# Values of six chunks computed with their router logits beside the shared expert, stored, and loaded in attention

## The chip, the cores and the metric

The kernel runs on one core of a Trainium2 chip. The metric is the device time of one execution in microseconds, the median over several. A profiled execution comes with it: its span is the time between the first and the last instruction that the profiler recorded.

## The reference

The input x is (4, 1024, 256) in float32, so there are 4096 tokens of width 256. Cut to what matters:

```python
xn = (x - mean(x)) / sqrt(var(x) + 1e-5)              # over the last axis

# attention, one head of width 256, softmax over all 1024 keys of a batch
q = xn @ Wq.T + bq ; k = xn @ Wk.T + bk ; v = xn @ Wv.T + bv
z = softmax(q @ k.T / 16) @ v

# mixture of experts on the same xn: 16 experts of hidden width 128, the best 2 of each token
gates = softmax(xn @ Wg.T) ; scores, inds = top_k(gates, 2) ; scores /= sum(scores)
y = sum over the 2 of scores * (silu(xn @ We_gate[e].T) * (xn @ We_up[e].T)) @ We_down[e].T
# shared expert of hidden width 512, scaled by a gate of its own
shared = (silu(xn @ Ws_gate.T) * (xn @ Ws_up.T)) @ Ws_down.T
out = x + z + y + sigmoid(xn @ Wsg.T) * shared
```

## The kernel before

The 4096 tokens are 32 tiles of 128 rows, or 8 chunks of 4 tiles (a chunk is also a group g of 512 queries; two groups make one batch). Every float32 product is made of float32r halves: an operand is split into a high part and a remainder (`HI`, `LO`), and `product` (line 803) issues three passes for each half of the contraction, so six matmuls for a width of 256 and 24 for the 1024 keys.

There is no scheduler. `plan()` (line 103) writes one list of steps by hand. Each engine's program walks that list and issues what belongs to it in that order; semaphores carry the dependences. So the list sets each engine's order, and an engine that waits in one step holds up all its later ones.

The stages, in order:

- **Shared expert.** Steps 0 to 45 of `shared`, each a pair of gate and up products (`gate_up`, 12 matmuls of 512 columns) or a pair of tiles of the down projection (`down`, `down_second`, 24 matmuls of 256 columns). The table `beside` hangs the small work on them, in three places of a step: ahead, amid, behind. Among it: `tokens_in` (8 transposes of a chunk's normalized rows into `xT`), `logits` (4 matmuls of 512 columns with the router, padded to 128 columns, as the stationary operand, into a transposed form), `logits_turn` (4 transposes back, the two halves of the sum added by VectorE, DVE), `best_experts`, and then the routing itself. `expert_split` splits the experts' weights as they arrive, on ScalarE (ACT, high part) and GpSimd (POOL) or DVE (remainder). `xT` of each chunk is stored to `keys` in device memory.
- **Routed experts.** 79 blocks of 128 gathered rows, in 40 pairs (`blk_turn`, `blk_gate_up`, `blk_hidden`, `blk_down`). At its end stands the first work of attention.
- **Attention.** `heads` (b, u) makes the mixed queries of 512 tokens (12 matmuls of 512 columns), `values` (b, u) the values of four tiles (24 matmuls of 256 columns), both from `xT` loaded back as `xbT`. A group g has four pairs of key tiles: `scores` (g, pair), 12 matmuls of 512 columns, and `scores_copy` on ACT; `scores_max` on DVE finds the greatest key for each query, `tops` shifts it and POOL reduces it over the partitions, `spread` and `less` subtract it on DVE, `probs`, `probs_hi` (ACT) and `probs_lo` (DVE) make the weights of a tile of queries, and `weigh` (24 matmuls of 258 columns, 256 values and the sum) with `weigh_sum` on DVE ends it. A group's `weigh` stands one group later. `rows` is the sum of the routed experts' rows on DVE (`rows_in`), followed on POOL by the gather of the rows of the tile three further on into the same of three buffers (`YR`), which waits for that `rows_in`.

`scores_copy` of pair 0 of a group waits for all four `less` of the group before. `heads`, `values` and `scores` share two pairs of PSUM banks in turn (`ring_banks`). `tokens_in`, `logits`, `logits_turn` and others share two single banks in turn (`turn_bank`): a step waits until the one before it in its bank has been read. `weigh` (n) waits for `weigh_sum` (n-2) before it overwrites its bank.

Of the kernel before, what the change touches and what calls it, by code (L numbers as in the profile page):

```python
# [18 lines left out]
P = 128  # L19
# [3 lines left out]
KD = D // P  # L23
# [15 lines left out]
RLO = 32  # L39
# [63 lines left out]
def plan():  # L103
# [31 lines left out]

    shared = []
    for c in range(NCH):
        shared += [(up, c, 0), (up, c, 1)]
        if c > 0:
# [11 lines left out]
        3: ([], [], [("stats", 4)]),  # L151
        4: ([("weights_lo", 5)],
            [("logits", 1), ("logits_turn", 0), ("weights_hi", 5), ("root", 2, 3), ("invert", 2, 3)],
            []),
        5: ([("logits_turn", 1), ("best_experts", 0)], [], []),
# [3 lines left out]
        9: ([], [("tokens_in", 3), ("stats", 7)], []),  # L159
        10: ([], [("logits", 2)], []),  # L160
        11: ([("expert_load", 1), ("root", 4, 5, 6, 7), ("logits", 3), ("invert", 4, 5, 6, 7)],
            [("logits_turn", 2)],
            []),
        12: ([("norm", 4)], [], [("logits_turn", 3)]),
        13: ([], [("tokens_in", 4)], [("norm", 5), ("expert_split", 1)]),
        14: ([], [("logits", 4)], []),
        15: ([("norm", 6)], [("tokens_in", 5)], [("expert_split", 2)]),
        16: ([], [("tokens_in", 6), ("norm", 7)], []),
        17: ([("logits", 5)], [("logits_turn", 4), ("best_experts", 1)], []),
        18: ([("tokens_in", 7)], [("expert_split", 3)], []),  # L170
        19: ([("logits_turn", 5), ("logits", 6)], [], [("best_experts", 2)]),
        20: ([], [("logits_turn", 6), ("logits", 7)], [("expert_split", 4)]),
        21: ([], [("logits_turn", 7)], [("best_experts", 3)]),
# [33 lines left out]
    for b in range(PAIRS + 2):  # L207
        if 0 < b < PAIRS:
            steps.append(("blk_gate_up", b))

        if b == PAIRS:
            steps.append(("heads", 0, 0))
        if 0 < b <= PAIRS:
            steps.append(("blk_hidden", b - 1))
        if b == PAIRS + 1:
            steps.append(("values_first", 0, 0))
# [29 lines left out]
    ahead = {1: split("heads", 1, 1), 2: split("heads", 2, 0), 3: split("heads", 2, 1), 4: split("heads", 3, 0),  # L246
# [10 lines left out]
    for g in range(GROUPS):  # L257
# [18 lines left out]
        if g in (1, 3):  # L276
            steps.append(("keys_load", g // 2 + 2))
# [85 lines left out]
def build(nc, x, bv, Wqkv, bqk_in, Wr, We, Ws, const_f, const_b, out):  # L363
# [4 lines left out]
    with ctx:  # L368
# [230 lines left out]
        def inverse_of(c):  # L599

            return 5 * [c in group for group in ROOTS].index(True) + 4
# [1132 lines left out]
```

## Time and profile before

| | |
|---|---|
| median of 3 runs | 510.38 us (509.88 to 511.83) |
| profiled execution, its own time | 509.88 us |
| its span | 508.1 us |
| PE busy | 502.8 us |
| DVE busy | 402.9 us |
| ACT busy | 279.9 us |
| POOL busy | 197.9 us |

Busy time is the union of an engine's instructions. Matmuls are pipelined and overlap in it, so what one costs is read from the distance between starts, not from its duration. A piece of the chain of waits gives when it began, how long it lasted, and what ran; a bracket in a timeline row is the engine's idle time before the row and what ended it.

### The profile page before, as it was taken

Reading aid. Unit: us, or ns where it says so; the run is one execution under the profiler, and the core shown is the slowest. Engines: PE = TensorE matmul, PEld = TensorE weight load, DVE = VectorE, ACT = ScalarE, POOL = GpSimd, SP = SyncE. Lnnn points to the kernel's source line nnn. Section 1 sums busy time; section 2 is a strip of 40 time slices with the busy share of each in tenths; the row PEclk is TensorE's granted clock in tenths of the full one; section 3 lists DMA queues with packets and bytes.
Section 4 is the critical chain, followed back from the end, with each engine's and each line's share of the span. In section 5 each row is a group of like instructions: output and inputs, shape, how many; then the busy total and the mean of one; then the engine's idle time right before and its main releaser. Section 6 shows DMA issues by size and latency. Waiting matters only on the chain.

```text
span 508.1 us, 9935 instructions
## 1 busy us (share of the span) xinstructions
PE 502.8 (99%) x3411; PEld 461.3 (91%) x3411; DVE 402.9 (79%) x847; ACT 279.9 (55%) x466; POOL 197.9 (39%) x178
## 2 busy tenths in 40 slices
PE   8999999999999999999999999999999999999997
PEld 6898988888889999999999889999989898989897
DVE  6989457899997677677776288997969797887997
ACT  4787884246655465555555547473826454553652
POOL 0001021111005777777760370454363436262740
PEclk9999999999999999999999999999999999999999
DMA  8937176111213565786575740632253323121212
GB/s 303 411 133 281 79 288 243 42 54 33 62 63 109 179 190 181 228 305 205 188 153 137 249 137 21 199 112 63 85 159 122 83 62 84 33 78 47 82 55 74
DMA packets 31185, 71.27 MB, mean 140 GB/s; under 512 B 5313, under 2 KB 9793, under 8 KB 30113
## 3 DMA queue, kind: packets, MB, share of 16 engines
q1 hardware_dynamic: 23840, 51.80, 28.6%
q0 software_dynamic: 6864, 18.75, 14.4%
q8 instruction: 30, 0.49, 0.4%
q10 hardware_dynamic: 432, 0.09, 0.1%
q14 instruction: 19, 0.15, 0.1%
HBM read 43.34 MB, written 27.28 MB: 139 GB/s over the span
## 4 chain that ended last, share of the span: by engine, by line
PE 89%; DVE 7%; issue 2%; ACT 1%; DVEq 0%
PE ps L808 55%; PE ps L1018 11%; PE ps L948 7%; PE ps L814 6%; PE ps L1050 6%; PE ps L903 1%; PE ps L861 1%; PE ps L965 1%; DVE pT L1334 1%; DVE acc L1431 1%; PE ps L912 1%; DVE place_hot L1523 1%; DVE sil L1412 1%; DVE hT L1334 1%; DVE probs_f L1675 0%
## 5 line engine op out<-in xcount | busy, mean ns | idle before, releaser
L795 POOL DMA_INDIRECT rows_y<-ytab,slot x64 | 81.1, 1267 | 87.6 <-DVE acc L1690 67.9
L765 POOL DMA_INDIRECT blk_x<-rows,row x79 | 83.7, 1059 | 48.4 <-DVE row L1538 22.7
L808 PEld LDWEIGHTS ps<-vv,pT 128*128 128x128 f32 x768 | 94.6, 189 | 1.3 <-DVE pT L1334 0.3
L808 PE MATMUL ps<-vv,pT 128*128 128x258 f32 x768 | 95.6, 283 | 0.1
L808 PE MATMUL ps<-xT,shared_w 128*128 128x512 f32 x384 | 92.7, 394 | 0.4 <-DVE sil L1412 0.2
L808 PEld LDWEIGHTS ps<-xT,shared_w 128*128 128x128 f32 x384 | 70.7, 188 | 15.5 <-issue 0.8
L808 PE MATMUL ps<-qT,xbT_hi 128*128 128x512 f32 x256 | 79.1, 390 | 0.0
L1018 PE MATMUL ps<-expert_w,blk_xT 128*128 x474 | 66.0, 288 | 0.3 <-DVE blk_xT L1334 0.3
L1018 PEld LDWEIGHTS ps<-expert_w,blk_xT 128*128 128x128 f32 x474 | 58.9, 190 | 0.6 <-issue 0.6
L1322 ACT ACTIVATE probs_f<-probs_f 128x1024 f32<-128x1024 f32 x32 | 33.8, 1057 | 41.3 <-DVE probs_f L1675 41.2
L1128 ACT ACTIVATE scored_t<-ps 128x1024 f32<-128x1024 f32 (+1 forms) x33 | 32.4, 996 | 43.6 <-PE ps L808 39.4
L808 PEld LDWEIGHTS ps<-qT,xbT_hi 128*128 128x128 f32 x256 | 47.0, 188 | 9.2
L749 POOL TENSOR_TENSOR expert_w<-stage_e,expert_w 128x768 fp32r<-128x768 f32 x7 | 13.4, 1911 | 105.6 <-ACT expert_w L1128 105.6
L808 PE MATMUL ps<-qT,xbT_lo 128*128 128x512 f32 x128 | 50.0, 390 | 0.0
L1334 DVE TENSOR_TENSOR blk_xT<-ps,blk_xT 128x512 fp32r<-128x512 f32 (+1 forms) x40 | 27.3, 683 | 20.0 <-ACT blk_xT L1128 20.0
L948 PE MATMUL ps<-shared_w,hT 128*128 128x256 f32 x336 | 42.8, 285 | 0.0
L948 PEld LDWEIGHTS ps<-shared_w,hT 128*128 128x128 f32 x336 | 41.2, 191 | 0.2
L1334 DVE TENSOR_TENSOR pT<-probs_f,pT 128x1024 fp32r<-128x1024 f32 x32 | 39.1, 1223 | 0.8 <-ACT pT L1128 0.8
L1675 DVE TENSOR_TENSOR probs_f<-scored_t,less_wide 128x1024 f32<-128x1024 f32 x32 | 38.5, 1220 | 0.4
L1050 PE MATMUL ps<-expert_w,blk_hT 128*128 x237 | 38.0, 296 | 0.0
L1128 ACT ACTIVATE pT<-probs_f 128x1024 fp32r<-128x1024 f32 x32 | 33.9, 1059 | 0.8
L1252 ACT ACTIVATE blk_sil<-ps 128x256 f32<-128x256 f32 (+1 forms) x40 | 15.3, 382 | 32.9 <-PE ps L1018 32.9
(167 smaller groups left out, 858.2 us busy)
## 6 DMA issues: line engine op xcount, KB each, us to landing
ytab<-blk_y SPq DMA_DIRECT2D x40, 256.0 KB, 2.8
keys<-xT SPq DMA_DIRECT2D x8, 1024.0 KB, 6.1
stage_e<-in_experts SPq DMA_DIRECT2D x16, 384.0 KB, 3.1
rows<-xn SPq DMA_DIRECT2D x8, 512.0 KB, 3.2
xbT_hi<-keys SPq DMA_DIRECT2D x8, 512.0 KB, 6.2
xbT_lo<-keys SPq DMA_DIRECT2D x8, 512.0 KB, 7.3
out<-acc SPq DMA_DIRECT2D x32, 128.0 KB, 1.8
acc<-in_x SPq DMA_DIRECT2D x7, 512.0 KB, 9.2
```

The lines of the kernel that those rows point to most:

```text
L765: e.indirect_dma_start(out=blk_x[:, q, n, :], out_offset=None, in_=rows, in_offset=bass.IndirectOffsetOnAxis(ap=row[:, 2 * b + n:2 * b + n ...
L795: e.indirect_dma_start(out=rows_y[:, r, k, :], out_offset=None, in_=ytab, in_offset=bass.IndirectOffsetOnAxis(ap=slot[:, k, i:i + 1], axis=0),
L808: ins = e.matmul(dst, stationary(p, k), moving(q, k), start=(n == 0), stop=(n == total - 1))
L814: ins = e.transpose(dst[:, n * P:(n + 1) * P], s, ident)
L948: ins = e.matmul(ps[:, b, (n % 2) * D:(n % 2 + 1) * D], hT[:, p, j, n * P:(n + 1) * P], shared_w[:, q, 2 * KD * SH + j * D:2 * KD * SH + ( ...
L1018: ins = e.matmul(ps[:, 2 + r, n * D:(n + 1) * D], blk_xT[:, r, p, (n * KD + k) * P:(n * KD + k + 1) * P], weights(b, n, q, k * 2 * HID, 2 ...
L1050: ins = e.matmul(ps[:, 6 + r, n * D:(n + 1) * D], blk_hT[:, r, p, n * P:(n + 1) * P], weights(b, n, q, 2 * D, D), start=(at == 0), stop=(a ...
L1128: e.activation(hi, src, ACT.Copy).then_inc(done, 1)
L1252: e.activation(blk_sil[:, r, 0:used(b), :], gu[:, 0:used(b), 0:HID], ACT.Silu).then_inc(blk_silu, 1)
L1322: e.activation(probs_f[w][:, :, :], probs_f[w][:, :, :], ACT.Exp).then_inc(exp_made, 1)
L1334: e.tensor_tensor(lo, src, hi.bitcast(F32), ALU.subtract).then_inc(done, 1)
L1675: e.tensor_tensor(probs_f[w][:, :, :], scored_t[:, 0:KT, t * P:(t + 1) * P], less_wide[:, t * P:(t + 1) * P].unsqueeze(1).to_broadcast([P, ...
```

## The change

The 24 tiles of chunks 2 to 7 get their values and their 18 logits from one product (`vals`, six matmuls of 274 columns, the tokens as the stationary operand, w_v beside the router as the moving one) in the shared expert's stage. ACT copies the logits and the values out of PSUM, POOL splits the values, and SP stores them (`vals` in device memory, three buffers, `VR`). Chunks 0 and 1 get their logits alone in that form (`logits`, 24 matmuls of 18 columns each); the transposed logits, their turning back and the addition are gone. The weights for this are split in a step of their own, and SP loads w_v for it among the first loads. The values of batches 1 to 3 are loaded in attention (`vals_load`); batch 0 still computes its own.

`heads` (0,0) moves a block pair earlier and is whole there, `values` (0,0) is in two halves at the stage's end, group 0 holds `heads` (0,1) and `values` (0,1) and nothing of batch 1, and each later group makes the heads of the next one (before, two groups ahead). In group 0 the four `rows` stand after `probs_lo`; before, two of them stood among the scores. The last pair of group 0's scores is copied in two halves, as the last group's was.

```diff
+VRC = D + RC
+VR = 3
+NATIVE = 2
+STORED = TILES - NATIVE * CT
...
-        0: ([("router_split",), ("root", 1), ("stats", 2)], [("weights_hi", 3), ("invert", 1)], []),
-        1: ([("norm", 1), ("weights_lo", 3)], [("logits", 0)], []),
+        0: ([("root", 1), ("stats", 2)], [("weights_hi", 3), ("invert", 1)], []),
+        1: ([("norm", 1), ("weights_lo", 3)], [("value_split",)], [("keys_store", 0)]),
...
         if g == 0:
-            steps += [*split("heads", 0, 1), ("heads", 1, 0), ("tops", g), ("heads_split", 1, 0),
-                      ("values", 0, 1), *spread(g), ("values", 1, 0), ("less", new),
...
+            steps += [("tops", g), *split("heads", 0, 1), ("values", 0, 1), *spread(g), ("less", new),
+                      ("values_split", 0, 1), ("probs", new), ("less", new + 1), *spread_second(g), ("probs_hi", new),
+                      ("probs", new + 1), ("probs_lo", new), ("less", new + 2), ("probs_hi", new + 1), ("less", new + 3),
+                      ("probs_lo", new + 1), *rows(new), *rows(new + 1), *rows(new + 2), *rows(new + 3)]
...
+                elif kind == "vals":
+                    t, i = CT * (a[0] - NATIVE) + a[1], CT * a[0] + a[1]
+                    e.wait_ge(vals_lo, t + 1)
+                    e.dma_start(vals[i // BT - 1, :, :, i % BT, :], vals_out[:, t % VR, :, :].bitcast(F32)).then_inc(
+                        vals_stored[t % VR], 16)
...
+                elif kind == "vals_load":
+                    b, r = a[0], a[0] % 2
...
+                    for part in (HI, LO):
+                        e.dma_start(vv[:, r, part, :, 0:D].bitcast(F32), vals[b - 1, :, part, :, :]).then_inc(vals_loaded[r], 16)
...
+                elif kind == "vals":
+                    t = CT * (a[0] - NATIVE) + a[1]
+                    r = t % VR
+                    e.wait_ge(vals_copied, t + 1)
+                    if t >= VR:
+                        e.wait_ge(vals_stored[r], 16 * (t // VR))
+                    e.tensor_copy(vals_out[:, r, HI, :], vals_f[:, r, :]).then_inc(vals_hi, 1)
+                    e.wait_ge(vals_hi, t + 1)
+                    e.tensor_tensor(vals_out[:, r, LO, :], vals_f[:, r, :], vals_out[:, r, HI, :].bitcast(F32),
+                                    ALU.subtract).then_inc(vals_lo, 1)
...
                     for n in range(CT):
-                        ins = e.transpose(ps[:, bank, n * P:(n + 1) * P], logits_t[:, n * P:(n + 1) * P], ident)
-                    ins.then_inc(logits_made, 1)
+                        product(ps[:, bank, n * RC:(n + 1) * RC], lambda p, k: xT_of(c)[:, p, k, n * P:(n + 1) * P],
+                                lambda q, k: value_w[:, q, k, D:VRC], logits_made)
+                elif kind == "vals":
+                    c, n = a
+                    if n == 0:
+                        e.wait_ge(xT_lo, KD * (c + 1))
+                    product(ps[:, turn_bank(("vals", c, n)), 0:VRC], lambda p, k: xT_of(c)[:, p, k, n * P:(n + 1) * P],
+                            lambda q, k: value_w[:, q, k, :], valued)
...
+                elif kind == "vals":
+                    t, i = CT * (a[0] - NATIVE) + a[1], CT * a[0] + a[1]
+                    bank = before[("vals", *a)][0]
+                    e.wait_ge(valued, t + 1)
+                    copied(logits_sb[:, i, :], ps[:, bank, D:VRC], logits_copied)
+                    if t >= VR:
+                        e.wait_ge(vals_lo, t - VR + 1)
+                    copied(vals_f[:, t % VR, :], ps[:, bank, 0:D], vals_copied)
```

PE, in the shared expert's stage, from the first `gate_up` to the end of chunk 1's logits, before (`xT_56` and `xT_57` are the transposed tokens of chunks 0 and 1, `xn` their normalized rows, `cf` the identity):

```order
L808 MATMUL ps<-xT_56,shared_w 128x512 x24
L903 MATMUL ps<-xT_56,router 128x512 x4
L808 MATMUL ps<-xT_56,shared_w 128x512 x12
L814 MATMUL ps<-cf,xn_63 128x128 x8
L808 MATMUL ps<-xT_56,shared_w 128x512 x12
L808 MATMUL ps<-xT_57,shared_w 128x512 x12
L903 MATMUL ps<-xT_57,router 128x512 x4
L912 MATMUL ps<-cf,logits_t 128x128 x4
L808 MATMUL ps<-xT_57,shared_w 128x512 x12
L912 MATMUL ps<-cf,logits_t 128x128 x4
```

The same stretch of PE in the changed kernel:

```order
L862 MATMUL ps<-xT_56,shared_w 128x512 x36
L868 MATMUL ps<-cf,xn_63 128x128 x8
L862 MATMUL ps<-xT_56,shared_w 128x512 x12
L862 MATMUL ps<-value_w,xT_56 128x18 x24
L862 MATMUL ps<-xT_57,shared_w 128x512 x12
L862 MATMUL ps<-value_w,xT_57 128x18 x24
L862 MATMUL ps<-xT_57,shared_w 128x512 x12
```

The third `gate_up` now follows the first two with nothing between, and the logits stand later and are many short matmuls.

ACT, in steps 12 to 14 of the same stage, in the changed kernel (`xT_60` is chunk 4's, `xn_62` and `xn_63` the two buffers of normalized rows):

```order
L1195 ACTIVATE xn_62<-acc,negm,rstd 128x256 x4
L1175 ACTIVATE logits_sb<-ps 128x18
L1175 ACTIVATE vals_f<-ps 128x256
L1175 ACTIVATE logits_sb<-ps 128x18
L1175 ACTIVATE vals_f<-ps 128x256
L1175 ACTIVATE hT<-sil 128x512 x2
L1175 ACTIVATE logits_sb<-ps 128x18
L1175 ACTIVATE vals_f<-ps 128x256
L1175 ACTIVATE logits_sb<-ps 128x18
L1175 ACTIVATE vals_f<-ps 128x256
L1175 ACTIVATE xT_60<-ps 128x512 x2
L1195 ACTIVATE xn_63<-acc,negm,rstd 128x256 x4
```

Before, the same place held one copy of chunk 2's turned logits (`logits_sb`, 128x72) ahead of and one behind the normalization; now each tile has two copies, and two tiles stand straight ahead of the tokens' copies.

DVE, from the first spread of group 0 to the first key maximum of group 1, before:

```order
L1675 TENSOR_TENSOR probs_f_104<-scored_t,less_wide 128x1024
L1667 TENSOR_TENSOR less_wide<-shift_wide,top_keys 128x256
L1334 TENSOR_TENSOR vv<-ps,vv 128x4x256
L1675 TENSOR_TENSOR probs_f_105<-scored_t,less_wide 128x1024
L1334 TENSOR_TENSOR pT_97<-probs_f_103,pT_97 128x1024
L1675 TENSOR_TENSOR probs_f_103<-scored_t,less_wide 128x1024
L1334 TENSOR_TENSOR pT_98<-probs_f_104,pT_98 128x1024
L1690 SCALAR_TENSOR_TENSOR acc<-rows_y,score,acc 128x256 x4
L1334 TENSOR_TENSOR pT_99<-probs_f_105,pT_99 128x1024
L1647 TENSOR_TENSOR top_keys<-scored_t 128x1024
```

and in the changed kernel:

```order
L1727 TENSOR_TENSOR probs_f_106<-scored_t,less_wide 128x1024
L1719 TENSOR_TENSOR less_wide<-shift_wide,top_keys 128x256
L1390 TENSOR_TENSOR pT_99<-probs_f_105,pT_99 128x1024
L1727 TENSOR_TENSOR probs_f_107<-scored_t,less_wide 128x1024
L1727 TENSOR_TENSOR probs_f_105<-scored_t,less_wide 128x1024
L1390 TENSOR_TENSOR pT_100<-probs_f_106,pT_100 128x1024
L1742 SCALAR_TENSOR_TENSOR acc<-rows_y,score,acc 128x256 x8
L1390 TENSOR_TENSOR pT_101<-probs_f_107,pT_101 128x1024
L1699 TENSOR_TENSOR top_keys<-scored_t 128x1024
```

The split of batch 1's values (the row with `vv`) is gone, and the rows of four tiles (eight instructions) stand where two did.

## Rows read from the trace of the kernel before

**Rows 1.** The page: PE's busy time, and the chain's shares by engine.

```profile
PE 502.8 (99%) x3411; PEld 461.3 (91%) x3411; DVE 402.9 (79%) x847; ACT 279.9 (55%) x466; POOL 197.9 (39%) x178
...
PE 89%; DVE 7%; issue 2%; ACT 1%; DVEq 0%
```

**Rows 2.** Windows: stretch, span, busy us of PE, PEld, DVE, ACT, POOL, clock, DMA, GB/s.

```profile
43.76:89.00 45.24, 45.24 (x276) 39.80 (x274) 27.81 (x106) 31.94 (x63) 5.63 (x3) 1.00 0.60 229
389.00:417.00 28.00, 28.00 (x182) 25.66 (x182) 23.25 (x35) 14.47 (x16) 12.34 (x11) 1.00 0.23 66
```

**Rows 3.** The chain of waits: start, us, what.

```profile
16.40 0.91 PE ps L903 x4
...
27.34 0.44 PE ps L912 x4
27.78 2.77 PE ps L808 x12
...
133.84 0.59 PE ps L997 x16
...
201.55 0.79 PE ps L1062 x8
...
282.31 196.81 PE ps L808 x1224
```

**Rows 4.** PE's timeline: first matmul of eight value tiles, and the one after them.

```profile
302.06 0.28 PE L808 MATMUL ps<-w_v,xbT_hi 128*128 128x256 f32 x1
...
307.81 0.40 PE L808 MATMUL ps<-qT,xbT_hi 128*128 128x512 f32 x1
```

**Rows 5.** DVE's timeline ahead of the third gate_up.

```profile
16.28 0.69 DVE L1412 TENSOR_TENSOR sil<-sil,ps 128x512 f32<-128x512 f32 x1 [0.46 <-ACT sil L1194]
```

**Rows 6.** Timelines of ACT and POOL, and the DMA view: KB, us to landing.

```profile
274.19 0.38 ACT L1128 ACTIVATE blk_hT<-ps 128x256 fp32r<-128x256 f32 x1
...
6.73 0.40 POOL L744 COPY bq_wide<-bqk 128x256 f32<-128x256 f32 x1 [5.65 <-DMA bqk<-in_bqk]
...
62.90 1.85 POOL L749 TENSOR_TENSOR expert_w<-stage_e,expert_w 128x768 fp32r<-128x768 f32 x1 [20.26 <-ACT expert_w L1128]
...
ytab<-blk_y SPq DMA_DIRECT2D x40, 256.0 KB, 2.8
keys<-xT SPq DMA_DIRECT2D x8, 1024.0 KB, 6.1
```

**Rows 7.** Timelines, group 0 to group 1.

```profile
301.07 0.68 DVE L1659 TENSOR_TENSOR top_keys<-top_keys,shift_wide 128x512 f32<-128x512 f32 x1
...
309.07 1.23 DVE L1334 TENSOR_TENSOR vv<-ps,vv 128x1024 fp32r<-128x1024 f32 x1 [0.20 <-ACT vv L1128]
...
313.99 1.03 ACT L1128 ACTIVATE scored_t<-ps 128x1024 f32<-128x1024 f32 x1 [1.97 <-DVE probs_f L1675]
...
316.18 0.39 PE L808 MATMUL ps<-qT,xbT_hi 128*128 128x512 f32 x1
```

**Rows 8.** Timelines, group 1 to group 2.

```profile
314.95 1.92 DVE L1690 SCALAR_TENSOR_TENSOR acc<-rows_y,score,acc 128x256 f32<-128x256 f32 x4
...
325.16 0.69 DVE L1659 TENSOR_TENSOR top_keys<-top_keys,shift_wide 128x512 f32<-128x512 f32 x1
...
339.18 1.92 ACT L1128 ACTIVATE scored_t<-ps 128x1024 f32<-128x1024 f32 x2
...
338.52 0.28 PE L808 MATMUL ps<-vv,pT 128*128 128x258 f32 x1
...
341.42 0.39 PE L808 MATMUL ps<-qT,xbT_hi 128*128 128x512 f32 x1
```

**Rows 9.** The gathered rows: POOL's issues, and their landing.

```profile
316.22 1.04 POOL L795 DMA_INDIRECT rows_y<-ytab,slot  x1 [12.23 <-DVE acc L1690]
317.57 1.63 POOL L795 DMA_INDIRECT rows_y<-ytab,slot  x1 [0.31 <-issue]
...
DMA to landing us min/median/max: 2.8/3.3/6.7
```

More of the change, by code:

```diff
@@ L134, in down, with vals @@
         steps.extend(behind)
+    def vals(c, *tiles):
+        return [("vals", c, n) for n in tiles]
     shared = []
@@ L243, in probs @@
         return [("probs", n), ("probs_hi", n), ("probs_lo", n)]
-    ahead = {1: split("heads", 1, 1), 2: split("heads", 2, 0), 3: split("heads", 2, 1), 4: split("heads", 3, 0),
-             5: split("heads", 3, 1), 6: split("values", 3, 1)}
-    behind = {2: split("values", 1, 1), 3: split("values", 2, 0), 4: split("values", 2, 1), 5: split("values", 3, 0)}
+    ahead = {g: split("heads", *divmod(g + 1, 2)) for g in range(1, GROUPS - 1)}
     def spread(g):
@@ L253, in spread_second @@
         return [("spread_second", g), *([("shift_in", g + 2)] if g + 2 < GROUPS else [])]
-    steps += [("keys_load", 1), ("shift_in", 0), ("shift_in", 1), ("heads_second", 0, 0), ("heads_split", 0, 0), ("ones",), *split("values", 0, 0)]
+    steps += [("shift_in", 0), ("keys_load", 1), ("shift_in", 1), ("vals_load", 1), ("values_split", 0, 0), ("ones",)]
     steps += [("gather", i) for i in range(YR)]
@@ L267, in plan @@
             steps += [("probs", new - 1), ("probs_hi", new - 1)]
-        steps += [("scores_max", g, 1), *(rows(new) if g == 0 else [])]
+        steps += [("scores_max", g, 1)]
         if g == 1:
@@ L273, in plan @@
         else:
-            steps += [*(weigh(old) if g else []), *scores(g, 2), ("scores_max", g, 2), *(rows(new + 1) if g == 0 else [])]
+            steps += [*(weigh(old) if g else []), *scores(g, 2), ("scores_max", g, 2)]
         steps += [*scores(g, 3), ("scores_max", g, 3)]
@@ L322, in __init__ @@
                 turn += 2
-            elif kind in ("logits", "logits_turn", "counts", "rows_map"):
+            elif kind in ("logits", "vals", "counts", "rows_map"):
                 banks = [(("turn", turn % 2), step)]
@@ L446, in build @@
         r_xr = r_w + 4 * 4 * KD * D + PART
[L447 removed]
+        qT = [at(f"qT{n}", where, [P, 2, KD, CHUNK], F32R) for n, where in enumerate((r_xr, r_ew))]
         vv = at("vv", r_ew + 4 * PART, [P, 2, 2, BT, VC], F32R)
@@ L588, in build, with copied_upto, tops_upto @@
         ROWS_LAST = 16 * (NCH // 2)
-        LAST_PAIR = (GROUPS - 1, CT - 1)
+        HALVED = ((0, CT - 1), (GROUPS - 1, CT - 1))
+        def copied_upto(g, pair):
+            return nth[("scores", g, pair)] + sum((g, pair) >= both for both in HALVED)
+        def tops_upto(g):
+            return 4 * (g + 1) + sum(g >= both[0] for both in HALVED)
         LAST_SUMS = range(TILES - CT - 2, TILES - 2)
@@ L601, in inverse_of, with vals_stored_upto, logits_upto @@
             return 5 * [c in group for group in ROOTS].index(True) + 4
+        def vals_stored_upto(r, n):
+            return 16 * ((n - r + VR - 1) // VR)
+        def logits_upto(q):
+            return sum(1 if c < NATIVE else CT for c in range((q + 1) * QT // CT))
         def chunks_of(chunks):
@@ L1639, in vector_program @@
                         for half in range(2):
-                            e.wait_ge(scores_copied, nth[("scores", g, pair)] + half)
+                            e.wait_ge(scores_copied, copied_upto(g, pair) - 1 + half)
                             e.wait_ge(tops_found, at + half + 1)
@@ L1650, in vector_program @@
                         e.tensor_tensor(top_keys[:, :, :], top_keys[:, :, :], these, ALU.max).then_inc(tops_found, 1)
-                    if pair == CT - 1 and (g, pair) != LAST_PAIR:
+                    if pair == CT - 1 and (g, pair) not in HALVED:
                         e.wait_ge(tops_found, at + 1)
```

228 lines of the change are left out of this document (111 added, 117 removed).

## The prediction

> **What bounds the kernel now.** I read the page first. PE is busy for 502.8 of 508.1 us, and the chain of waits runs through PE for 89% of the span [rows 1]. That alone could be a busy time full of small gaps, so I read the pieces of the chain. From 282.31 us one piece on PE lasts 196.81 us without a break: nearly all of attention goes by PE alone [rows 3]. The windows say the same of the shared expert's stage (43.76 to 89.00, PE 45.24 of 45.24 us) and of a group and a half of attention (389 to 417, PE 28.00 of 28.00) [rows 2]. The next busiest is DVE: 27.81 of 45.24 us in the first, 23.25 of 28.00 in the second. So the reader is to see two things. What PE no longer does comes off the time almost one to one, as long as the others keep up; and in attention DVE is at 83%, so it does not take much to make PE wait for it there.
>
> **What PE no longer does.** One chunk's logits cost 4 matmuls in 0.91 us and 4 transposes in 0.44 us [rows 3]; eight chunks make 10.8 us. Eight value tiles, 48 matmuls of 256 columns, take from 302.06 to 307.81, which is 0.120 us each [rows 4]; the 144 for chunks 2 to 7 make 17.25 us. Together 28.05 us go.
>
> **What PE does instead.** 144 matmuls of 274 columns: 12 matmuls of 512 columns took 2.77 us, 0.231 each [rows 3], against 0.120 for 256, so a column costs 0.43 ns and 18 more cost 7.8 ns. 144 times 0.1276 is 18.4 us. Then 48 matmuls of 18 columns. The trace has none like them. The lower bound is the 16-bit kind: 16 matmuls of 80 columns in 0.59 us, 0.037 each; the upper bound is a matmul of 256 columns, 0.120. The nearest row is that of matmuls of a single column with 32-bit weights of 128 by 128, 8 in 0.79 us, 0.099 each [rows 3]: with one column nothing but the load of the weights is left, and these products load such weights for each matmul too. I take 0.10, 4.8 us in all (1.8 to 5.8). PE's work then changes by 18.4 + 4.8 - 28.05 = -4.85 us.
>
> The Trainium skill, in "TensorE: Matmul & The Clock Gate", section Back-to-back issue gap, gives a stream of matmuls as 81 ns at 128 columns and 131 ns at 512, and some 60 cycles, an issue floor of about 25 ns, for 1 to 64 columns. By that slope, 0.13 ns a column, the 18 added columns would cost 0.3 us in all where I have 1.1, and by the floor the 48 short ones 1.2 us where I have 4.8: the sum would be lower by 4.4 us. Our rows have 231 ns at 512 columns, so its spacing doesn't hold here for this type of data, and I stay with the rows.
>
> **The start.** The first chunk's logits leave their place ahead of the third `gate_up`, which ran at 17.31, behind 0.91 us of them [rows 3]. Without them PE is ready at 16.40, but that `gate_up` also waits for the first hidden product on DVE, which ends at 16.28 + 0.69 = 16.97 [rows 5]. So 0.57 us of the saving is lost to a wait whose cover is gone. The larger split of w_v with the router (548 columns for 36) stands on ACT and DVE one step later; the two steps that now precede the logits, 2.77 us each, cover it. The added load of 256 KB delays the later weights by less than a microsecond. I add 0.6 us.
>
> **The values beside the shared expert.** In 43.76 to 89.00 six chunks' logits go (8.1 us) and 18.4 us come, so the 24 tiles share some 55.5 us, 2.3 us a tile. ACT gets two copies a tile, at most 0.38 us each [rows 6], 18 us in all against 31.94 busy of 45.24 before [rows 2], less the logits' own copies: about 45 of 55.5. POOL gets a copy of 256 columns (0.40) and a subtraction, which at 1.85 us for 768 columns is some 0.62 [rows 6], 24 us in all. DVE gets nothing. Both engines fit. In order, the new wait on PE is that for the bank: where `tokens_in` follows two tiles of values (four places), its first half waits for the copies of the first of them. PE spends 0.77 us on the second tile, ACT 0.76 at most on the two copies of the first, so each place loses the hand-over and little more, 0.1 to 0.3 us. Behind the waiting transposes stands the next `gate_up`. The turned logits had such waits too. I add 0.3 us net (bounds 0 and 3). The routing needs chunk 7's logits; DVE gets them earlier after PE's last product than before, as no turn and addition follows, and that hides behind the same steps of PE, so nothing is gained or lost.
>
> **The end of the experts' stage.** `heads` (0,0) and `values` (0,0) have as many matmuls as before, a pair earlier, and stand as cover between the same waits. Zero; without that cover the last blocks would wait for their splits, at most 1 us.
>
> **The first two groups.** This is where the gain goes back, so I count it out, from the start of the first `scores`. PE before had `heads` (1,0) and `values` (1,0), 2.77 + 2.88 = 5.65 us, between group 0 and group 1; they are gone there. PE now: four pairs of scores 11.1, heads 2.8, values 2.9, two pairs of group 1 5.5, weigh(0) 2.9 (341.42 less 338.52) [rows 8]: it wants the third pair of group 1 at 25.2. That needs the copy of its pair 0, which needs the last `less` of group 0. Before, from the start of the step `tops` at 301.07 to the end of that copy at 313.99 + 1.03 it took 13.95 us, and DVE did batch 1's split in it, 1.23 plus 0.20 of idle [rows 7]. Without them it is 12.6. `tops` can start at 12.5 (11.1, a half copy of 0.6, a maximum of 0.7), so the copy ends at 25.1: just in time. (Before, it ended at 315.02 and was wanted at 316.18: 1.16 us of slack [rows 7].)
>
> Then the rows. DVE is through with the probabilities at 25.1 and sums the rows of four tiles, 0.96 each [rows 8]. The fourth needs the gather that POOL may start only after the first (26.05): 1.35 us to the second issue, then 3.3 to its landing [rows 9], 30.7. DVE waits 2.8 us there, until 30.7, with the remainders of tiles 2 and 3, the maxima and `tops` of group 1 queued behind, and is done with the rows at 31.65. To `tops` of group 1 it has five passes of 1.2, one of 0.7 and a `weigh_sum` of about 0.7, 7.4 in all: 39.05. From there to the end of the copy of group 2's first pair it took 325.16 to 339.18 + 0.96, 15.0 us [rows 8]: 54.0. PE wants its third pair of group 2 at 25.2 + 5.5 + 2.8 + 8.7 + 5.5 + 2.9 = 50.6 (two pairs, heads, three weighs, two pairs, a weigh). Before, with 5.65 us more of PE's work and the same time of DVE, it had 1.3 us to spare: 341.42 against 340.14. Now PE waits 3.4 us, a part of it already at weigh(3), which waits for DVE's `weigh_sum` of tile 1. So of the 5.65 us taken out there, 3.4 come back.
>
> **The later groups.** Each loses 2.88 us on PE and one split of 1.2 us on DVE. For a group of 28 us before [rows 2] that is 25.1 us of PE and 22.05 of DVE. DVE is still 3 us below. I add nothing, with 0 to 2.5 us as bounds (half a microsecond in each of five groups). The loads of values, 2 MB each, stand some two groups ahead of their first use.
>
> **The sum.** -4.85 + 0.6 + 0.3 + 3.4 = -0.55 us. The profiled execution took 509.88 us around its span of 508.1, so its successor would take 509.3; the median of the runs is 0.5 us above that execution, so 509.8 us.
>
> **The rivals.**
> - *DVE's slack is enough.* If the fourth tile's rows do not hold up DVE (the gather lands sooner, or the order leaves room), DVE is 2.8 us earlier, and PE waits 0.6 us. For it speaks that the shortest landing is 2.8 us; against it that the gather must still start after the first sum, and DVE has only 1.9 us of other rows to fill. 509.8 - 2.8 = 507.0 us. Chance 0.18.
> - *The short products are cheap.* If the weights' load hides, as for the 16-bit matmuls at 0.037 us, the 48 cost 1.8 us: 506.8 us. The page cited above gives 505.4. Against it stands the row of 0.099. Chance 0.09.
> - *The stores hold up the values* (the slower side). Three slots; a slot is busy for POOL's 1.02 us, about 0.4 for the issue, and the store's landing. With the 2.8 us of the 256 KB stores to `ytab` [rows 6] that is 4.2 over three, 1.4 us a tile, far below 2.3. But SP's stores of `keys`, 1 MB in 6.1 us, stand among them; were each landing 6.1 us, a tile takes 2.5 us, 0.2 more than PE, and over 24 tiles ACT and then PE's bank wait 4.8 us: 514.6 us. It decides above a landing of 5.5 us. For it speaks that DMA was at 0.60 there already and gets 6 MB more. Chance 0.14.
> - *DVE becomes the bound in every group*: 2.5 us and more, 512.3 to 514. Against it the 3 us of difference. Chance 0.08.
>
> **How the numbers follow.** The forecast has 0.5, its own range is 508 to 511.5. The rest, 0.01, is elsewhere. A change of 0.5% (2.55 us) is about what a measurement can tell. Below 507.8 lie the first two rivals, nearly whole, and a tail of the forecast: 0.29. Above 512.9 lie the third, most of the fourth, and a tail: 0.22. The range takes in both sides: 505.8 (the short products cheap, with a little of the first rival) to 514.2.
>
> **What the profile after would show.** The matmuls of 18 columns at about 0.10 us and those of 274 at 0.127; the third `gate_up` waiting for DVE at about 16.9; the stage of values some 10.5 us longer, with PE's idle time below 1 us; attention from its first scores to the end shorter by some 14 us; in group 0 DVE idle for 2 to 3 us on gathered rows, and PE waiting for 3 to 4 us in all before the third pair of group 2, for DVE's sum and for ACT's copy. I would be wrong if PE waits in every later group, if `vals_f` waits long for POOL, if the landing of `vals` goes beyond 5.5 us, or if DVE never waits for a gather.

## The result, and the profile after

The changed kernel is slower: 515.82 us, the median of four executions (514.65 to 517.17), against 510.33 for the kernel before (four, 509.88 to 511.83). The ratio is 1.0109, 95% interval 1.0094 to 1.0124. The forecast was 509.8 us with a range up to 514.2, so both the sign and the range missed. The profiled execution took 516.11 us, its span 514.2.

The page of the changed kernel: busy times, PE and its granted clock in 40 slices, and the chain's shares.

```profile
PE 505.7 (98%) x3394; PEld 462.6 (90%) x3395; DVE 396.9 (77%) x834; ACT 280.7 (55%) x495; POOL 223.1 (43%) x225
...
PE   8999999999999999999999999989999999999997
...
PEclk9979999999999999999999999998999999999999
...
PE 81%; DVE 11%; issue 3%; DMA 3%; ACT 2%; POOL 1%; ACTq 0%; DVEq 0%
```

Against [rows 1], PE is busy for 2.9 us more though it issues fewer matmuls, and the chain has 11% of DVE where it had 7%. The row to stop at is PEclk: a 7 in the third slice and an 8 in the 28th. In [rows 2] the clock was 1.00.

Windows of the changed kernel (stretch, span, busy us and count of PE, PEld, DVE, ACT, POOL, clock, DMA share, GB/s), from the first two chunks' logits to the first `down`, the stage of the values, and around a `weigh` of group 1:

```profile
23.56:26.15 2.59, 2.59 (x25) 2.59 (x24) 2.56 (x10) 0.46 (x1) 0.00 (x0) 1.00 1.06 437
26.15:30.58 4.43, 4.43 (x14) 3.48 (x14) 3.08 (x12) 1.46 (x3) 0.00 (x0) 0.61 0.62 257
30.58:33.18 2.60, 2.60 (x26) 2.60 (x24) 0.00 (x0) 0.00 (x0) 0.00 (x0) 1.00 0.00 0
33.18:37.59 4.41, 4.41 (x14) 3.47 (x14) 3.00 (x18) 4.03 (x7) 0.00 (x0) 0.61 0.32 89
37.59:43.34 5.75, 5.75 (x49) 5.75 (x48) 4.61 (x28) 3.55 (x6) 0.00 (x0) 1.00 0.22 88
50.53:107.56 57.03, 56.66 (x372) 51.52 (x371) 29.94 (x102) 38.49 (x98) 33.19 (x48) 1.00 0.78 281
336.00:346.30 10.30, 8.55 (x60) 7.83 (x59) 9.99 (x15) 2.28 (x3) 8.35 (x7) 1.00 0.55 157
346.30:352.00 5.70, 5.63 (x29) 5.45 (x30) 5.59 (x10) 4.09 (x5) 1.44 (x3) 0.70 0.86 302
```

Rows one and three are the 24 matmuls of 18 columns: 2.59 us, 0.108 each, PE never idle and PEld busy all along. Behind each stands one `gate_up` of twelve matmuls, which takes 2.77 us in [rows 3] and 4.42 here, at a clock of 0.61: most of it was granted at 1.2 GHz, the lower level, the rest at 2.4. Each of these two falls costs 1.65 us. In the mean clock of a span of 514 us one fall is 0.39 times 4.43 over 514, or 0.0034. The mean clock of every execution is recorded, so falls can be counted without a profile, though not placed: 0.990, 0.992, 0.993 and 0.990 in these four, two to three falls each. (A mean of 0.999 stands in executions of the kernel before too, the profiled one among them, and is not counted as a fall.)

Timelines of PE, DVE and ACT in the changed kernel (start, us; the bracket is the idle time before, and what ended it):

```profile
17.11 3.00 PE L862 MATMUL ps<-xT,shared_w 128*128 128x512 f32 x12 [0.63 <-DVE sil L1461]
...
68.39 1.06 PE L868 MATMUL ps<-cf,xn 128*128 128x128 f32 x8 [0.20 <-ACT vals_f L1175]
...
77.92 1.34 PE L868 MATMUL ps<-cf,xn 128*128 128x128 f32 x8
79.01 2.33 PE L862 MATMUL ps<-xT,shared_w 128*128 128x512 f32 x9
...
335.32 1.00 DVE L1742 SCALAR_TENSOR_TENSOR acc<-rows_y,score,acc 128x256 f32<-128x256 f32 x2 [2.75 <-DMA rows_y<-ytab,slot]
...
346.37 4.64 PE L862 MATMUL ps<-vv,pT 128*128 128x258 f32 x24 [1.82 <-DVE acc L1752]
...
357.22 1.92 ACT L1175 ACTIVATE scored_t<-ps 128x1024 f32<-128x1024 f32 x2
...
359.25 0.63 PE L862 MATMUL ps<-qT,xbT_hi 128*128 128x512 f32 x2
```

The third `gate_up` waits for DVE as forecast (0.63 us). The transposes of `tokens_in` behind two value tiles take 1.09 us, from 77.92 to 79.01, where 0.80 is what they take alone, and at 68.39 they wait for ACT's copy of a tile. DVE waits 2.75 us for the fourth tile's gathered rows (2.8 forecast). PE then waits 1.82 us for DVE's `weigh_sum`, and the 24 matmuls of that `weigh`, 2.9 us elsewhere, take 4.47 at a low clock. The last two rows are the copies of group 2's first two pairs of scores and PE's start on its third pair, without a wait. The DMA view has the new transfers (KB each, us from issue to landing):

```profile
vals<-vals_out SPq DMA_DIRECT2D x24, 256.0 KB, 3.0
vv<-vals SPq DMA_DIRECT2D x6, 1024.0 KB, 11.7
```

The stores land after 3.0 us in the median and 5.8 at most, so most are far below the 5.5 at which they would have held up the values; POOL waited for one twice, 1.6 us in all.

### The profile page after: what moved, and what is told of

Its sections match the earlier page's. It is cut to its first block, busy times and chain, and to the rows that moved or that the text cites. A ratio compares the mean times of both kernels' runs of the same rounds, so it can differ in the third digit from the quotient of the medians.

```text
span 514.2 us, 10011 instructions
## 1 busy us (share of the span) xinstructions
PE 505.7 (98%) x3394; PEld 462.6 (90%) x3395; DVE 396.9 (77%) x834; ACT 280.7 (55%) x495; POOL 223.1 (43%) x225
## 3 DMA queue, kind: packets, MB, share of 16 engines
HBM read 49.89 MB, written 33.57 MB: 162 GB/s over the span
## 4 chain that ended last, share of the span: by engine, by line
PE 81%; DVE 11%; issue 3%; DMA 3%; ACT 2%; POOL 1%; ACTq 0%; DVEq 0%
PE ps L862 51%; PE ps L1067 10%; PE ps L997 6%; PE ps L868 6%; PE ps L1099 5%; DVE pT L1390 2%; PE ps L1014 1%; DMA bqk<-in_bqk 1%; DVE probs_f L1727 1%; DMA blk_x<-rows,row 1%; DVE sil L1461 1%; DVE place_hot L1575 1%; POOL blk_x L819 1%; DMA rows_y<-ytab,slot 1%; DVE hT L1390 1%
## 5 line engine op out<-in xcount | busy, mean ns | idle before, releaser
L849 POOL DMA_INDIRECT rows_y<-ytab,slot x64 | 79.4, 1241 | 77.0 <-DVE acc L1742 57.3
L819 POOL DMA_INDIRECT blk_x<-rows,row x79 | 82.3, 1042 | 50.1 <-DVE row L1590 22.7
L862 PEld LDWEIGHTS ps<-vv,pT 128*128 128x128 f32 x768 | 95.7, 192 | 3.4 <-issue 2.0
L862 PE MATMUL ps<-xT,shared_w 128*128 128x512 f32 x384 | 96.2, 405 | 1.1 <-DVE sil L1461 0.9
L862 PEld LDWEIGHTS ps<-xT,shared_w 128*128 128x128 f32 x384 | 72.7, 194 | 17.0 <-issue 1.7
L1742 DVE SCALAR_TENSOR_TENSOR acc<-rows_y,score,acc 128x256 f32<-128x256 f32 x64 | 30.5, 481 | 3.9 <-DMA rows_y<-ytab,slot 2.7
```

The costliest lines, as they stand in the source:

```text
L819: e.indirect_dma_start(out=blk_x[:, q, n, :], out_offset=None, in_=rows, in_offset=bass.IndirectOffsetOnAxis(ap=row[:, 2 * b + n:2 * b + n ...
L849: e.indirect_dma_start(out=rows_y[:, r, k, :], out_offset=None, in_=ytab, in_offset=bass.IndirectOffsetOnAxis(ap=slot[:, k, i:i + 1], axis=0),
L862: ins = e.matmul(dst, stationary(p, k), moving(q, k), start=(n == 0), stop=(n == total - 1))
L1742: e.scalar_tensor_tensor(out=acc[:, i, :], in0=rows_y[:, r, k, :], scalar=score[:, k, i:i + 1], in1=acc[:, i, :], op0=ALU.mult, op1=ALU.ad ...
```

## The experiments

Two causes stood to be tested: that the short products themselves bring the clock down behind them, and that DVE's wait for the gathered rows is what stops PE in group 1 and brings the clock down there. Eleven more kernels were run. This is what they gave; the last column counts executions by their mean granted clock.

| run | median us (lowest to highest, n) | ratio to before (95%) | mean clock |
|---|---|---|---|
| changed kernel | 515.82 (514.65 to 517.17, 4) | 1.0109 (1.0094 to 1.0124) | .990 x2, .992, .993 |
| e1_wide | 512.75 (511.54 to 515.96, 9) | 1.0054 (1.0030 to 1.0077) | 1.000 x4, .997 x4, .996 |
| e3_rows | 516.98 (515.81 to 517.89, 4) | 1.0128 (1.0111 to 1.0145) | .997, .990 x2, .986 |
| e2_short | 512.88 (1) | | 1.000 |
| e2_wide | 513.10 (1) | | 1.000 |
| e5_two_short | 518.78 (518.13 to 519.35, 4) | 1.0166 (1.0149 to 1.0183) | .997 x2, .993 x2 |
| e6_late | 511.69 (509.67 to 513.37, 8) | 1.0028 (1.0011 to 1.0045) | 1.000 x2, .997 x4, .993 x2 |
| e7_wide_late | 510.11 (509.55 to 511.61, 10) | 0.9998 (0.9988 to 1.0008) | 1.000 x10 |
| e8_turned_late | 508.17 (507.90 to 508.48, 4) | 0.9958 (0.9942 to 0.9975) | 1.000 x4 |
| e9_split_late | 510.59 (509.92 to 510.93, 10) | 1.0000 (0.9989 to 1.0010) | 1.000 x8, .999 x2 |
| e10_long_short | 520.58 (517.78 to 522.55, 4) | 1.0198 (1.0152 to 1.0243) | .997, .993, .990 x2 |
| e10_long_wide | 516.55 (516.13 to 517.57, 4) | 1.0122 (1.0102 to 1.0143) | 1.000 x3, .999 |

The ratios are to the kernel before as it ran beside each: 510.60 us beside e1_wide, e3_rows and the two e2 runs (12 executions), 510.36 beside e5_two_short to e8_turned_late (17), 510.10 beside the e9 and e10 runs (13). Its mean clock was 1.000 in 39 of these 42 and 0.999 in three.

**The same products, wider (e1_wide).** In the changed kernel:

```diff
-                        product(ps[:, bank, n * RC:(n + 1) * RC], lambda p, k: xT_of(c)[:, p, k, n * P:(n + 1) * P],
-                                lambda q, k: value_w[:, q, k, D:VRC], logits_made)
+                        product(ps[:, bank, n * P:(n + 1) * P], lambda p, k: xT_of(c)[:, p, k, n * P:(n + 1) * P],
+                                lambda q, k: value_w[:, q, k, VRC - P:VRC], logits_made)
```

> The changed kernel with one edit: the logits of chunks 0 and 1 are products of 128 columns (110 value columns, not used, and the 18 of the router) where they had 18; ACT copies the same 18. As many matmuls, the same weights, the same places. Theory (the short products do so little work that the granted clock falls for the gate_up behind them, 4.4 us instead of 2.8): the 24 matmuls still take some 2.6 us, each gate_up behind them is back at 2.77 us at a clock of 1.00, and the kernel takes 3.3 us less than the changed one, 512.5. Rival (it is the pattern of reloading the weights for each matmul, or the pace of one matmul in 0.108 us, or what DMA does at that time): windows of 0.61 as before and 515.8 us.

It took 3.1 us less than the changed kernel, and the intervals of the two ratios do not touch. Its windows, the four that answer to the first four above:

```profile
23.32:25.95 2.63, 2.63 (x25) 2.62 (x24) 2.60 (x11) 0.47 (x1) 0.00 (x0) 1.00 1.06 435
25.95:28.77 2.82, 2.82 (x14) 2.31 (x14) 2.12 (x7) 1.46 (x3) 0.00 (x0) 1.00 0.90 375
28.77:31.40 2.63, 2.63 (x26) 2.63 (x24) 0.91 (x6) 0.00 (x0) 0.00 (x0) 1.00 0.07 28
31.40:34.22 2.82, 2.82 (x15) 2.31 (x14) 1.57 (x4) 2.45 (x5) 0.00 (x0) 1.00 0.11 13
```

As many matmuls, the same weights, the same 0.11 us each, and the clock stays at 1.00 behind them. DMA is as busy beside the stretches as in the changed kernel (1.06 and 0.07 for 1.06 and 0.00), so it is not that either. A product seven times as wide costs nothing at that pace and saves the fall. The wait in group 1 is still there (1.82 us at 342.83), with a fall behind it in the profiled execution. Falls are not the whole spread of the nine: two of the five with one took 515.7 and 516.0 us, the other three 512.6 to 514.4; where that difference went was not traced.

**Short products in the kernel before (e2_short, e2_wide, e5_two_short).** The added step, in the second with `P` for `RC`, in the third at two places:

```diff
+                elif kind == "filler":
+                    for n in range(CT):
+                        for k in range(KD):
+                            for p, q in PASSES:
+                                e.matmul(ps[:, 7, 0:RC], xT_of(0)[:, p, k, n * P:(n + 1) * P], router[:, k, 0:RC],
+                                         start=True, stop=True)
```

> The kernel before with 24 matmuls added and nothing else, between the products of the fourth step of the shared expert: 18 columns each, tokens of chunk 0 as stationary operand, the router as moving one, results not used. Theory (short products lower the clock for what follows): 2.6 us for the 24 and a window of 0.6 in the gate_up behind them, 1.6 us more, 514 to 514.6 in all. Rival (it needs something of the changed kernel, its DMA or its waits): the 2.6 us alone at a clock of 1.00 all through, 512.5 to 513.

> As the run before, with the 24 added matmuls 128 columns wide (the padded router). Both theories: 2.6 us for the 24. Theory of the short products: clock 1.00 all through and 512.5 to 513. Rival (the reloading of weights): the same low clock as with 18 columns, 514 or more.

The single runs told nothing apart: 512.88 with 18 columns, 513.10 with 128, and the clock at 1.00 behind both. The theory's own number for the short ones failed there. The profiled execution of e3_rows (below) showed the same: the short products of the changed kernel, and no fall behind them, while its other three executions have mean clocks down to 0.986. So the fall is not in every execution, and one execution can't decide about it. What follows rests on several executions of each kernel and on their clocks.

> The kernel before with two stretches of 24 matmuls of 18 columns, one between the products of the fourth and one between those of the fifth step of the shared expert, their results not used. One such stretch left the clock at 1.00 in its single run, so now the mean granted clock of every run is what counts. Theory (the short products lower the clock, not in every execution but in most): 5.2 us for the matmuls and up to 3.3 more, 516 to 519, mean clock of the span below 0.998 in most runs. Rival (the fall needs something else of the changed kernel, its waits of PE at the start or its loads): 1.00 in all runs and 515.5 to 516.

All four executions had one or two falls, and it took 8.4 us more than the kernel before. Windows of its profiled execution: the first stretch, the `gate_up` behind it, the second stretch, and what follows (the logits as in the kernel before, a `gate_up`).

```profile
23.66:26.26 2.60, 2.60 (x26) 2.60 (x24) 2.57 (x11) 0.21 (x1) 0.00 (x0) 1.00 1.02 416
26.26:29.12 2.86, 2.86 (x14) 2.33 (x14) 2.16 (x6) 1.23 (x2) 0.00 (x0) 1.00 0.57 241
29.12:31.74 2.62, 2.62 (x25) 2.62 (x24) 0.65 (x5) 0.00 (x0) 0.00 (x0) 0.99 0.00 0
31.74:34.30 2.56, 2.56 (x10) 2.07 (x10) 0.00 (x0) 0.00 (x0) 0.00 (x0) 0.50 0.00 0
34.30:37.52 3.22, 3.22 (x15) 2.62 (x14) 1.50 (x4) 2.52 (x4) 0.00 (x0) 0.87 0.00 0
```

Behind the first stretch the clock stayed, behind the second it fell to 0.50, with nothing of the changed kernel there. Up to the end of the next `gate_up` it took 5.78 us where e2_short, at a full clock, took 4.12 (29.45 to 33.57): 1.66 us for the fall. The rival, that it needs the changed kernel's waits or loads, is out.

**One long stretch (e10_long_short, e10_long_wide).** As e2_short and e2_wide, with 48 added matmuls in a row.

> The kernel before with 48 matmuls of 18 columns in a row between the products of the fourth step of the shared expert, results not used: one stretch of 5.2 us, twice as long as the one that left its single run at a clock of 1.00. Theory (a longer stretch is seen surely): a fall in every run, mean clock 0.997 or lower, 5.2 + 1.7 to 3.3 us, 517 to 519. Rival (a single stretch doesn't do it, it needs two): clock 1.000 and 515.6.

> As the run before with the 48 added matmuls 128 columns wide. Theory: clock 1.000 in all runs and 510.4 + 5.2 = 515.6 us. If reloading the weights for each matmul lowers the clock, this one is as slow as the one with 18 columns.

Windows of the stretch and of the `gate_up` behind it, of the short one, then of the wide one:

```profile
23.80:30.41 6.61, 6.61 (x49) 6.60 (x48) 5.41 (x20) 0.88 (x2) 0.00 (x0) 0.79 0.64 266
30.41:35.12 4.71, 4.71 (x13) 3.72 (x14) 0.00 (x0) 0.60 (x1) 0.00 (x0) 0.57 0.00 0
```

```profile
23.61:28.92 5.31, 5.31 (x49) 5.30 (x48) 4.58 (x15) 0.88 (x2) 0.00 (x0) 1.00 0.81 333
28.92:31.75 2.83, 2.83 (x14) 2.31 (x14) 0.83 (x6) 0.60 (x1) 0.00 (x0) 1.00 0.01 3
```

With 18 columns the clock falls within the stretch itself (6.61 us for what takes 5.31 with 128) and stays low in the `gate_up` (4.71 for 2.83), 3.2 us for the two. All four executions have a mean clock below 1.00, by two of them as much as three falls, and at 520.58 us it is slower than the 517 to 519 expected. With 128 columns none of four shows a fall. The two medians are 4.0 us apart. The reloading of weights, which both have in common, is not the cause by itself. The wide one took 1.1 us more than its 5.3 us of matmuls; where these went was not traced.

**The rows back in their old place (e3_rows).** In the changed kernel:

```diff
-        steps += [("scores_max", g, 1)]
+        steps += [("scores_max", g, 1), *(rows(new) if g == 0 else [])]
...
-            steps += [*(weigh(old) if g else []), *scores(g, 2), ("scores_max", g, 2)]
+            steps += [*(weigh(old) if g else []), *scores(g, 2), ("scores_max", g, 2), *(rows(new + 1) if g == 0 else [])]
...
-                      ("probs_lo", new + 1), *rows(new), *rows(new + 1), *rows(new + 2), *rows(new + 3)]
+                      ("probs_lo", new + 1), *rows(new + 2), *rows(new + 3)]
```

> The changed kernel with one edit: the sums of the routed rows of tiles 0 and 1 stand again among group 0's scores, where they stood before the change, and only those of tiles 2 and 3 behind the remainders. Theory (DVE's 2.75 us of waiting for the fourth tile's gathered rows is handed on to PE, 1.82 us ahead of a weigh of group 1 and 1.7 us more by a lower clock behind that wait): no idle time of DVE there, no wait and no clock below 1.00 in group 1, 3.5 us less than the changed kernel, 512.3; if DVE is later at the scores' maxima of group 0 by the two sums moved there, up to 1.9 us of it come back as a wait of PE for the copy of group 1's first pair. Rival (PE would be held in group 1 anyway by the order of DVE's passes): the wait only moves, under 1 us gained.

Nothing gained: 516.98. The place where the rows stood before is too early now. The timelines of DVE and PE show it:

```profile
315.21 1.00 DVE L1742 SCALAR_TENSOR_TENSOR acc<-rows_y,score,acc 128x256 f32<-128x256 f32 x2 [3.47 <-DMA rows_y<-ytab,slot]
...
323.45 0.70 PE L862 MATMUL ps<-qT,xbT_hi 128*128 128x512 f32 x2 [3.04 <-DVE qT L1669]
```

and the window behind PE's wait:

```profile
323.40:330.00 6.60, 6.55 (x22) 5.06 (x23) 5.98 (x7) 3.70 (x4) 1.60 (x2) 0.74 0.30 98
```

The first gather waits for the experts' last stores and is issued at 307.85, 4.2 us after the first scores (303.66); in the kernel before it was 286.57, 0.9 us after them (285.69), since parts of batch 0's heads and values stood between the last expert's products and the scores. So the first gathered rows land only at 315.2. DVE waits for them with the maxima behind it, PE 3.04 us for DVE, and the clock falls to 0.74 behind that wait. The theory missed: the wait in group 1 did go, but a longer one stood 20 us ahead of it. The rival's outcome came (the wait moved, nothing was gained), but not for its reason: DVE was late for the gather's issue, not for the order of its passes in group 1, as the next run shows.

**The fourth tile's rows later (e6_late).** In the changed kernel:

```diff
-                      ("probs_lo", new + 1), *rows(new), *rows(new + 1), *rows(new + 2), *rows(new + 3)]
+                      ("probs_lo", new + 1), *rows(new), *rows(new + 1), *rows(new + 2)]
...
         if g == 1:
-            steps.append(("probs_lo", new - 1))
+            steps += [("probs_lo", new - 1), *rows(new - 1)]
```

> The changed kernel with one edit: the sum of the routed rows of group 0's fourth tile stands in group 1, behind the remainders of the probabilities, so that DVE has that work to do while the rows are gathered. Theory (DVE's wait for these rows is what PE's wait in group 1 and the low clock behind it come from): DVE idle below 0.3 us there, PE's 1.82 us gone, clock 1.00 from 336 to 352, 3.5 us less than the changed kernel: 512.3. Rival (DVE is short of time in groups 0 and 1 anyway, so the wait goes to another place): under 1 us gained, 515 or more.

4.1 us less than the changed kernel. Not all of it is the gather's: the clocks count about one fall an execution here, where the changed kernel had two to three. DVE's timeline in it:

```profile
328.03 2.83 DVE L1742 SCALAR_TENSOR_TENSOR acc<-rows_y,score,acc 128x256 f32<-128x256 f32 x6
330.78 1.22 DVE L1390 TENSOR_TENSOR pT<-probs_f,pT 128x1024 fp32r<-128x1024 f32 x1
331.92 1.22 DVE L1699 TENSOR_TENSOR top_keys<-scored_t 128x1024 f32<-128x1024 f32 x1
333.13 1.23 DVE L1390 TENSOR_TENSOR pT<-probs_f,pT 128x1024 fp32r<-128x1024 f32 x1
334.27 1.04 DVE L1742 SCALAR_TENSOR_TENSOR acc<-rows_y,score,acc 128x256 f32<-128x256 f32 x2
```

Three passes fill the time that the gather needs, and no row has a bracket. Its windows, the `gate_up` behind the second short stretch and the 16 us in which PE had waited:

```profile
31.46:35.88 4.42, 4.42 (x14) 3.48 (x14) 3.01 (x18) 4.04 (x7) 0.00 (x0) 0.61 0.29 89
...
336.00:352.00 16.00, 16.00 (x109) 14.85 (x108) 15.52 (x22) 7.99 (x9) 9.57 (x9) 1.00 0.75 230
```

PE is busy for 16.00 of 16.00 us at a full clock there. What remains in the profiled execution is the fall behind the short products; the mean clocks of the eight come to one fall on average. From the first scores to the end it takes 509.5 - 303.0 = 206.5 us, against 514.2 - 304.7 = 209.5 in the changed kernel.

**Both, and two other forms (e7_wide_late, e8_turned_late, e9_split_late).**

> The edits of the two runs that widen the first two chunks' logits to 128 columns and put the fourth tile's rows later, together. If both causes are separate they add up: 515.8 - 3.1 - 3.5 = 509.2 us, 1.4 below the kernel before, clock 1.00 all through. If the wait only moves: 512 or more.

The two edits together give 510.11 and a clock of 1.000 in ten of ten: the kernel before, within 0.1%. The expected 509.2 had a fall in group 1 in every execution; in e1_wide there was one in five of nine. That these were in group 1 fits with none in ten here, though only one of them was profiled. So the later rows give 2.6 us there (512.75 to 510.11; 2.9 by the two ratios) and not 3.5.

> The changed kernel with the fourth tile's rows later, and with each of the two stretches of 24 short products cut into two of 12, in four steps of the shared expert with a gate_up or a down between them. The same number of matmuls of 18 columns. Theory (what lowers the clock is that short products stand in a row for 2.6 us, not how many there are): mean clock 1.000 in nearly all runs and 510.1 us, like the wide form with the later rows. Rival (it is their number, or a matmul of 18 columns wherever it stands): falls in most runs and 511.7, as with the later rows alone.

```diff
-        3: ([], [("logits", 0)], [("stats", 4), ("keys_store", 1)]),
+        3: ([], [("logits", 0, 0)], [("stats", 4), ("keys_store", 1)]),
...
-                    for n in range(CT):
+                    for n in range(2 * half, 2 * half + 2):
```

510.59 us, no fall in ten: 1.1 us less than e6_late with the same 48 short products. The kernel with 48 in a row, run beside it, fell in four of four. It is that they stand in a row, not that they are there. Three of its four stretches of 12 also stand one or two steps later than their products did, which was not tested by itself.

The last, e8_turned_late, is the best kernel of the study. It makes the logits of the first two chunks in the form that the kernel before had, with 128 columns of the joint weights as the stationary operand:

```diff
-                    for n in range(CT):
-                        product(ps[:, bank, n * RC:(n + 1) * RC], lambda p, k: xT_of(c)[:, p, k, n * P:(n + 1) * P],
-                                lambda q, k: value_w[:, q, k, D:VRC], logits_made)
+                    product(ps[:, bank, :], lambda p, k: value_w[:, p, k, VRC - P:VRC],
+                            lambda q, k: xT_of(c)[:, q, k, :], summed_t)
+                elif kind == "logits_turn":
...
+                    for n in range(CT):
+                        e.transpose(ps[:, bank, n * P:(n + 1) * P], logits_t[:, n * P:(n + 1) * P], ident).then_inc(
+                            logits_made, 1)
```

> As the run before, but the logits of chunks 0 and 1 are six matmuls of 512 columns (128 columns of the joint weights as the stationary operand), copied and turned back by four transposes, in place of 24 matmuls: 1.39 + 0.35 = 1.74 us for 2.63 each. Theory (the number of matmuls with their own weights is what the form of the first two chunks costs): 1.8 us less than the wide form with the later rows, 507.4. Rival (PE has to wait for ACT's copies between the two parts, as the hidden work beside them is short): no less than it, 509 or more.

PE's timeline in it:

```profile
23.37 1.56 PE L864 MATMUL ps<-xT,value_w 128*128 128x512 f32 x6
24.76 2.89 PE L864 MATMUL ps<-xT,shared_w 128*128 128x512 f32 x12
27.49 0.60 PE L965 MATMUL ps<-cf,logits_t 128*128 128x128 f32 x4
27.85 1.64 PE L864 MATMUL ps<-xT,value_w 128*128 128x512 f32 x6
29.32 2.89 PE L864 MATMUL ps<-xT,shared_w 128*128 128x512 f32 x12
```

1.39 us for the six products and 0.36 for the four transposes, without a wait: 508.17 us, 0.42% below the kernel before. That is what the values' move is worth here with the two losses found above taken away; the wait of the third `gate_up` (0.59 us here) is still in it.

## Why the prediction was wrong, point by point

PE's work by stages in the profiled executions. The forecast's terms stand beside what the stage took, after less before:

| stage | forecast us | measured us |
|---|---|---|
| start to the first `down` | +2.7 (4.8 + 0.6 - 2.7) | 37.59 - 30.75 = +6.8 |
| to chunk 7's logits | +10.6 (18.4 - 8.1 + 0.3) | 107.56 - 37.59 less 88.91 - 30.75 = +11.8 |
| to the first scores | 0 | 197.17 - 196.78 = +0.4 |
| attention | -13.85 (3.4 - 17.25) | 209.5 - 222.4 = -12.9 |
| sum | -0.55 | +6.1 |

**The step that failed** is "I take 0.10, 4.8 us in all (1.8 to 5.8)". The price of a short product was read right as a spacing, 0.108 us measured, and wrong as a price. PE was busy with loading weights (PEld 2.59 of 2.59 us), with 18 columns of work behind each load, and the lower clock behind the two stretches cost 3.3 us more in this execution. So the 48 cost 5.2 + 3.3 = 8.5 us, above my upper bound. That bound, a matmul of 256 columns at 0.120, had seemed safe because a shorter one cannot take longer itself; it said nothing of what it does to the next. That it is the columns is shown by e1_wide and the pair of e10_long_short and e10_long_wide; that they must stand in a row, by e9_split_late. Why the same stretch brings the clock down in one execution and not in the next stays open. The Trainium skill, "TensorE: Matmul & The Clock Gate", section HAM oscillation, tells of the clock falling where the engine waits for DMA between bursts of matmuls. In group 1 this case's trace agrees in part: the clock was 0.70 behind a wait of 1.82 us, but that wait was for DVE, and shorter than those the section tells of. Behind the short products PE had been busy for 2.60 of 2.60 us, which the section does not speak of. The Trainium skill, "TensorE: Matmul & The Clock Gate", section LDWEIGHTS, gives the load of P columns of weights as P / 1.2 ns; for 128 columns that is an estimate of 107 ns, and the 0.108 us measured agrees. The floor of 25 ns that I had weighed does not hold here.

**The values beside the shared expert** were mis-sized by 1.2 us. A matmul of 274 columns takes 0.129 us (0.1276 forecast), 0.2 us over the 144. "Each place loses the hand-over and little more, 0.1 to 0.3 us" was right, with 0.29 us at 77.92 to 79.01, but in the sum I put 0.3 us for all four places together instead of four times that. ACT and POOL kept up, as forecast: 38.5 and 33.2 busy of 57.0.

**The first two groups.** DVE's wait for the fourth gather (2.75 for 2.8) was read right, and so was the way through DVE and ACT: the copy of group 2's first pair ended at 357.22 + 0.96 = 358.18, 53.5 us after the first scores, for 54.0. But that PE lost 3.4 us there, as forecast, is luck. It waited 1.82 us, and the low clock behind the wait, which I had not seen coming, cost 1.6 more. So PE came to its third pair at 54.5 us, after the copy, and did not wait for it; without the fall it would have come at 52.9 and waited about half a microsecond, 2.4 us in all (an estimate from these rows). e6_late shows that the loss is due to that one gather: 3.0 us of attention came back, and at the same place PE waits 0.34 us for ACT. My rival "DVE's slack is enough" had 2.8 for it.

**The rest.** The third `gate_up`'s wait (0.63) and the later groups (no wait of PE in them) were right; the end of the experts' stage was 0.4 us worse than nothing. The slower side that I gave a chance, the stores, did not happen: they landed after 3.0 us in the median, and the slow-down had another cause. Sum of the misses: 3.3 for the clock and 0.4 for the short products themselves, 1.2 in the values' stage, 0.4 with the experts, 0.9 in attention, and 0.4 spread over the start, 6.6 us in all, from -0.55 to +6.1. The 0.9 in attention stands beside a loss of PE there that has the forecast's size; it was not traced, and e6_late has about as much (206.5 - 222.4 = -15.9, with a wait of 0.34, for -17.25).

## What to carry to other kernels

Price a short product by what it does to the clock behind it too: before a stretch of narrow matmuls with full weights each, ask whether the narrow side can be made the stationary one, the product widened at the same pace, or the stretch cut up between wide work. Where a sum waits for a gather, put it behind work that the engine has anyway, and count from the issue that its buffer allows, not from the place in the list. When executions differ, count the mean granted clocks of several: one profile showed a fall that was not always there, and another missed one that mostly was.

## What the runs showed of the hardware

A matmul of 18 columns and one of 128, each with new 32-bit weights of 128 by 128, follow the one before it after 0.108 and 0.110 us. Stretches of 24 narrow ones (2.6 us), PE busy all along, were often followed by the lower clock: in e5_two_short and e6_late, with two stretches in each of their 12 executions, the mean clocks come to 14 falls for 24 stretches, if all of them stood behind the stretches. 48 in a row brought it down in four of four. The wide ones did so in none of e7_wide_late's ten, and 12 narrow ones at a time between wide work in none of e9_split_late's ten. Behind a wait of PE of 1.8 us the clock was low in the profiled execution of e1_wide, and five of its nine had a fall. A fall behind 24 narrow matmuls or behind that wait cost 1.6 to 1.7 us in each profile that shows one, and was over within 4.5 us; behind 48 the clock was low for longer, 3.2 us in all.
